# Conv-attention-MoE layer on one core: folded transform, idle matmuls, row spread moved in a DMA queue, a new order at the end

## The chip, the cores and the metric

One NeuronCore of a Trainium2 chip runs the whole layer in one launch; the other cores are idle. The metric is the device time of one execution in microseconds (us), taken as the median of several executions; lower is better. The engines named below are TensorE (PE: matmuls, and PEld: its weight loads), VectorE (DVE), ScalarE (ACT), GpSimd (POOL) and SyncE (SP), which here only issues transfers. Each engine works through its own instructions in order and waits on semaphores for the others.

## What is computed

Four images x of 192 channels by 16 x 16 pixels, all float32. In short (the helper functions are those of the reference):

```python
x = conv(x)              # fft2 over the view [B,16,16,192], first 9 columns of modes kept,
                         # two complex block layers (8 blocks of 24) with relu and softshrink,
                         # irfft2, plus x
t = to_tokens(x)                                   # [4, 256, 192]
t = t + attention(layernorm(t))                    # 12 heads of 16
t = t + moe(layernorm(t))
x = from_tokens(t)                                 # [4, 192, 16, 16]

def moe(xf):
    shared = expert(xf, swg, swu, swd)             # silu(x@wg) * (x@wu) @ wd, 192 -> 384 -> 192
    probs = softmax(xf @ w_gate + expert_bias)     # 16 experts
    p, i = top_k(probs, 2); p = p / sum(p)
    return shared + sum_k p_k * expert_{i_k}(xf)
```

## The kernel before

The program is written by hand, engine by engine, in four stages. Between engines there are only semaphores; the order in each engine's block is the order of execution.

**Transform and convolution (0 to 34 us).** PE multiplies the pixels by a table of cosines and sines (`fwd`, 128 x 576) to get the modes of each image: for each of 8 units `u`, 8 matmuls with 144 columns (L1112), two halves `k` of the 256 pixels accumulated. Then follow the block layers (L1126, L1140, L1145), the inverse transform (L1160), the turn into tokens (L1172), a bias row `out_bias` (L1249) that needs nine small transfers `ld_attn`, and the projections of attention. SP issues all the set-up transfers one after the other, from L412 to L454, between 0.7 and 29.3 us; the last of `ld_attn` is the expert bias at L448. DVE negates the imaginary halves of the weights `w1` and `w2` (L814) after the second image; PE waits for that (`negated`) before L1126.

**Attention (41 to 121 us).** A quad is 4 heads of one image, 12 quads in all. Queries and keys are projected two quads at a time (`project_pair(p)`), ACT adds their bias (`dense_rows(p)`, L677, semaphore `dense_ready`), and SP then copies them with `spread_rows(p)` (L481) from a dense layout into every second row of `qk_sb`. Quad 0 takes a short way; pair 0 serves quads 1 and 2, pair 1 serves quads 3 and 4, and so on. `spread_rows(p)` is in SP's queue between the loads of the expert weights, which are 14.2 MB in 6 groups of gate and up weights (`load_gate_up`, L464) and 4 groups of down weights (`load_down`, L468). PE's loop runs `n` over 24 half quads: scores of half quad `n` (L1296), then the row maxima of half quad `n + 3` (`pair_for_max`, L1267), then other work. So the maxima of half quad 6, the first of quad 3, are taken in iteration `n = 3`, and there PE waits for the rows of `spread_rows(1)`. DVE reduces each bank of maxima (L860), PE transposes them (`maxima_rows`, L1281), DVE shifts the queries.

**Routing (121 to 142 us).** Logits, the two best experts, a rank of each token inside its expert (`rank_and_count`, `base`), a chain of DVE instructions up to `is_part` (L999), then `slot_tokens` (L1473) and the first gathers. The shared expert is computed in 6 units of gate and up matmuls (`shared_gate_up(u)`, L1430 with all 128 rows and L1435 with the 64 that remain; units 0 to 2 for the first two images); pieces of units 0 to 2 stand between the steps of the routing.

**Experts and tail (142 to 243 us).** A loop over tiles of 128 slots, then units 3 to 5 of the shared expert, `shared_down` (L1444), and the reading back of the routed rows (`read_back`, 8 transfers from SP and ACT). For each of 8 token tiles DVE adds two weighted rows to the tokens (`mix`, L1079 and L1081), adds the shared part (`shared_rows`, L976), PE transposes the sums (`out_columns`, L1597, 16 transposes), ACT copies them out of PSUM (L798) and SP stores each image (L509).

The lines of SP's queue on which most depends are these:

```python
load_gate_up(*GU_GROUPS[0])      # experts 0 to 2, 1.77 MB
load_down(*DN_GROUPS[0])         # experts 0 to 3, 1.18 MB
spread_rows(0)
sp.wait_ge(S["tok_ready"], B)
load_down(*DN_GROUPS[1])         # experts 4 to 7, 1.18 MB
spread_rows(1)                   # two transfers of 0.13 MB
spread_rows(2)
load_gate_up(*GU_GROUPS[1])
```

Of the kernel before, what the change touches and what calls it, by code (L numbers as in the profile page):

```python
# [55 lines left out]
SPECTRAL = 2 * 2 * 768 + 3 * N + 4 * C + 3 * B * C + GROUPS * 2 * GC + 2 * GROUPS * B * MODES + B * (2 * C + IM - GC) + GROUPS * 129 + 4 * MODES  # L56
# [22 lines left out]
FILL_SET = 2  # L79


def constants():

    h, w = np.meshgrid(np.arange(H), np.arange(W), indexing="ij")
    k1, k2 = np.meshgrid(np.arange(H), np.arange(WF), indexing="ij")
# [13 lines left out]
        forward.reshape(2, 128, 2 * MODES).transpose(1, 0, 2).reshape(128, -1),  # L99
# [15 lines left out]
F_INV = F_FWD + 2 * 2 * MODES  # L115
# [8 lines left out]
def program(nc, a, out):  # L124
    ctx = ExitStack()
    with ctx:
# [51 lines left out]
        pix = carve(B * (2 * C + IM - GC)).rearrange("p (b c) -> p b c", b=B)  # L178
        w1 = carve(GROUPS * 128).rearrange("p (q r o) -> p q r o", q=GROUPS, r=2)
        b1 = carve(GROUPS)  # L180
        fwd = carve(2 * 2 * MODES).rearrange("p (k m) -> p k m", k=2)
# [18 lines left out]
        after_xT = at[0]  # L200
        probs = probs_flat.rearrange("p (s h k n) -> p s h k n", s=2, h=QUAD, k=2)
# [84 lines left out]

        gu_e = lambda e: main[:, bass.ds(e * GU, GU)]
# [6 lines left out]
        names = """ld_fwd ld_const ld_w1 ld_w2 ld_res ld_attn ld_qkv ld_shared ld_gu ld_dn  # L294
# [10 lines left out]
        mixed half_mixed outT_done outT_ready stored""".split()  # L305
# [28 lines left out]
        def shared_down_bank(u):  # L334
            return bank[(3, 1, 7, 6)[u]]

# [58 lines left out]
        def load_pixels(queue, b):  # L395
            queue.dma_start(pix[:, b, 0:2 * C].rearrange("p (k c) -> p k c", k=2),
                            a["x"][b].rearrange("c h w -> (c h w)").rearrange("(k p c) -> p k c", k=2, p=128)).then_inc(ld_pix[b], 16)
# [13 lines left out]
        def _(sp):  # L411
            sp.dma_start(fwd, a["tables_f32"][:, F_FWD:F_INV].rearrange("p (k m) -> p k m", k=2)).then_inc(S["ld_fwd"], 16)  # L412
# [70 lines left out]

            load_gate_up(*GU_GROUPS[0])
            load_down(*DN_GROUPS[0])
            spread_rows(0)
# [20 lines left out]
            for b in range(B):  # L507
                sp.wait_ge(S["outT_ready"], b + 1)
                sp.dma_start(out[b].rearrange("(k p) h w -> p k (h w)", k=2), out_T[0:CH, b]).then_inc(S["stored"], 16)  # L509
            sp.wait_ge(S["stored"], 16 * B)  # L510
# [3 lines left out]
        def _(pool):  # L514
# [3 lines left out]
            nc.gpsimd.memset(pix[:, :, 2 * C:], 0.0).then_inc(S["zeroed"], 1)  # L518
# [107 lines left out]
        def _(act):  # L626
# [169 lines left out]
            for b in range(B):  # L796
                act.wait_ge(S["outT_done"], b + 1)
                act.activation(out_T[0:CH, b, :, :], bank[b][0:CH, :].rearrange("p (k n) -> p k n", k=2), ACT.Copy).then_inc(S["outT_ready"], 1)  # L798
# [3 lines left out]
        def _(dve):  # L802
            vec = nc.vector
            vec.memset(eps_col, EPS).then_inc(S["eps_set"], 1)

            for b in range(B):
# [3 lines left out]
                if b == 1:  # L810

                    for w, loaded, count in ((w1, "ld_w1", 10), (w2, "ld_w2", 9)):
                        dve.wait_ge(S[loaded], 16 * count)
                        vec.tensor_scalar(w[IM:, :, 0, :], w[IM:, :, 0, :], -1.0, None, ALU.mult).then_inc(S["negated"], 1)  # L814
# [260 lines left out]
            def mix(t):  # L1075

                a, b = (tok, tok_b) if t < NT // 2 else (tok_b, tok)
# [8 lines left out]
            for t in range(NT // 2):  # L1086
# [543 lines left out]
```

## Times and profile before

| | before |
|---|---|
| median of 3 executions | 242.12 us (242.01 to 247.29) |
| the profiled execution | span 242.7 us |
| PE busy, share of the span | 93% |
| DVE, ACT, POOL busy | 62%, 47%, 32% |
| chain that ended last, by engine | PE 81%, DVE 6%, DMA 5%, ACT 4%, issue 2% |
| moved by DMA | 27.67 MB, mean 114 GB/s |

The profile is of one execution. A row of the timeline gives the start, the time from the first start to the last end of a merged run of instructions, engine, line, operation and tiles; in square brackets stands the idle time before it and who ended it. A float32 matmul shows as two records. "SPq" and "ACTq" rows are transfers as they are issued; when they land is in the table of DMA issues. PEclk is the granted clock of TensorE in tenths of 2.4 GHz, so that 5 is 1.2 GHz; the chip records only changes, and before the first change the row shows full clock whatever it was.

### The profile page before, as it was taken

What the parts mean: (1) busy time and instruction counts of PE and PEld (TensorE: products, weight loads), DVE (VectorE), ACT (ScalarE), POOL (GpSimd) and SP (SyncE); (2) the same over time, 40 slices, a digit from 0 to 9 for tenths busy, and PEclk for the clock granted to TensorE, in tenths of its full rate; (3) what the DMA queues carried; (4) which work ended last, traced back from release to release, by engine and by line L of the source; (5) the groups of instructions that cost most, each with busy time, mean ns of one, the idle gap of its engine ahead of it and who ended that gap; (6) DMA issues with size and microseconds to landing.
All of it is one profiled execution on the core that took longest, in us unless ns stands there. A gap on an engine that the chain in (4) does not pass through costs nothing.

```text
span 242.7 us, 5781 instructions
## 1 busy us (share of the span) xinstructions
PE 225.0 (93%) x1968; PEld 147.8 (61%) x1968; DVE 150.7 (62%) x353; ACT 113.3 (47%) x199; POOL 76.7 (32%) x119
## 2 busy tenths in 40 slices
PE   2999999599999999999889999999999999998982
PEld 2989876376666667677574655555555555553371
DVE  0217768344888898878767866565666566652383
ACT  0354046134445344434545357575757565655103
POOL 7003007000000072183510344565656565531000
PEclk9999999857999999999999999999999999999999
DMA  7971499900766895900750011111111111211524
GB/s 192 224 165 26 116 295 233 285 16 13 219 177 172 263 265 173 278 14 24 228 134 0 15 50 36 50 49 49 49 49 49 49 49 49 51 32 35 165 99 130
DMA packets 28099, 27.67 MB, mean 114 GB/s; under 512 B 7788, under 2 KB 26796, under 8 KB 28076
## 3 DMA queue, kind: packets, MB, share of 16 engines
q1 hardware_dynamic: 23372, 21.40, 32.4%
q0 software_dynamic: 2304, 4.72, 6.9%
q10 hardware_dynamic: 2400, 1.26, 2.2%
q8 instruction: 13, 0.21, 0.4%
q14 instruction: 10, 0.08, 0.1%
HBM read 22.49 MB, written 3.44 MB: 107 GB/s over the span
## 4 chain that ended last, share of the span: by engine, by line
PE 81%; DVE 6%; DMA 5%; ACT 4%; issue 2%; SPq 0%; ACTq 0%; DVEq 0%
PE grid L1531 11%; PE grid L1296 9%; PE bank L1557 9%; PE grid L1538 7%; PE bank L1314 4%; PE bank L1547 4%; PE bank L1160 3%; PE bank L1331 3%; PE bank L1267 3%; PE grid L1112 3%; DMA main<-main 2%; PE grid L1430 2%; PE bank L1281 2%; PE grid L1444 2%; PE bank L1126 2%
## 5 line engine op out<-in xcount | busy, mean ns | idle before, releaser
L750 ACT ACTIVATE main<-down_all 128x576 f32 x42 | 28.6, 684 | 27.3 <-PE bank L1557 26.1
L1046 DVE COPY main<-main 128x1152 f32 x41 | 31.7, 785 | 15.5 <-issue 13.8
L716 ACT ACTIVATE main<-grid 128x1024 f32<-128x1024 f32 x24 | 24.5, 1023 | 32.2 <-PE grid L1296 32.2
L582 POOL DMA_INDIRECT main<-xhat_rows,main x21 | 26.3, 1254 | 24.6 <-PE bank L1517 12.6
L1531 PE MATMUL grid<-main 128*64 128x384 f32 x160 | 29.8, 488 | 0.3 <-DVE main L1030 0.3
L1267 PE MATMUL grid<-main 32*128 32x256 f32 x132 | 29.8, 434 | 0.0
L1296 PE MATMUL grid<-main 32*128 32x256 f32 x192 | 27.8, 420 | 0.8 <-ACT main L716 0.6
L590 POOL DMA_INDIRECT pair_rows<-main x19 | 20.4, 1072 | 25.6 <-DVE main L1036 23.8
L860 DVE TENSOR_REDUCE main<-grid 128x2 f32<-128x512 f32 x33 | 21.8, 685 | 4.8 <-PE grid L1267 4.1
L1557 PEld LDWEIGHTS bank<-main 128*64 128x64 f32 x228 | 16.3, 136 | 12.3 <-ACT main L750 9.6
L1557 PE MATMUL bank<-main 128*64 128x192 f32 x228 | 22.7, 333 | 0.1
L1296 PEld LDWEIGHTS grid<-main 32*128 32x128 f32 x192 | 17.4, 196 | 7.8 <-issue 6.8
L1267 PE MATMUL bank<-main 32*128 32x256 f32 x60 | 18.7, 435 | 1.5 <-DMA main<-main 1.5
L1030 DVE TENSOR_TENSOR main<-main,grid 128x384 f32<-128x384 f32 x20 | 11.1, 555 | 13.8 <-ACT main L756 13.8
L559 POOL TENSOR_SCALAR main<-main 128x2 f32<-128x2 f32 x3 | 0.7, 221 | 56.6 <-DVE main L842 56.6
L1267 PEld LDWEIGHTS grid<-main 32*128 32x128 f32 x132 | 17.4, 200 | 0.5 <-issue 0.5
L1538 PE MATMUL grid<-main 64*64 64x384 f32 x160 | 17.5, 508 | 0.0
L1531 PEld LDWEIGHTS grid<-main 128*64 128x64 f32 x160 | 12.8, 137 | 7.7 <-issue 4.0
L860 DVE TENSOR_REDUCE main<-bank 128x2 f32<-128x512 f32 x15 | 10.3, 684 | 6.1 <-PE grid L1267 5.5
L1314 PE MATMUL bank<-main 128*32 128x256 f32 x192 | 12.8, 384 | 1.2 <-issue 1.1
L1547 PEld LDWEIGHTS bank<-cf,main 128*128 128x128 f32 x57 | 5.9, 141 | 11.4 <-issue 10.8
L1267 PEld LDWEIGHTS bank<-main 32*128 32x128 f32 x60 | 11.0, 202 | 2.2 <-DMA main<-main 1.7
(200 smaller groups left out, 399.1 us busy)
## 6 DMA issues: line engine op xcount, KB each, us to landing
down_all<-wd SPq DMA_DIRECT2D x4, 1152.0 KB, 9.3
main<-wg SPq DMA_DIRECT2D x4, 576.0 KB, 4.1
main<-wu SPq DMA_DIRECT2D x4, 576.0 KB, 6.2
main<-wg SPq DMA_DIRECT2D x4, 288.0 KB, 7.0
main<-wu SPq DMA_DIRECT2D x4, 288.0 KB, 8.1
main<-main SPq DMA_DIRECT2D x8, 128.0 KB, 2.7
main<-x SPq DMA_DIRECT2D x1, 768.0 KB, 6.2
main<-wg SPq DMA_DIRECT2D x2, 384.0 KB, 3.6
```

The costliest lines, as they stand in the source:

```text
L582: pool.indirect_dma_start(xg[:, t % 2, :], None, xhat_rows, bass.IndirectOffsetOnAxis(ap=slot_token[:, t:t + 1].bitcast(U32), axis=0)).the ...
L590: pool.indirect_dma_start(pair_rows, bass.IndirectOffsetOnAxis(ap=slot_pair[:, t:t + 1], axis=0), y_out[:, t % 2, :], None).then_inc(y_sto ...
L716: act.activation(probs[:, quad % 2, 2 * (n % 2):2 * (n % 2) + 2, :, :].rearrange("p h k n -> p h (k n)"), grid[:, score_banks(n), :], ACT. ...
L750: act.activation(w_dn[:, p, h, :], dn_e(expert(t, h)), ACT.Copy).then_inc(S["w_dn_ready"], 1)
L860: vec.tensor_reduce(negmax[:, g % QUADS, :, 64 * pair + 32 * h + SHIFT_ROW], max_bank(n, h).rearrange("p (q n) -> p q n", q=2), AX.X, ALU. ...
L1046: vec.tensor_copy(w_gu[:, p, h, :], gu_e(expert(t, h))).then_inc(S["w_gu_ready"], 1)
L1267: last = mm(max_bank(n, h)[:, qh * N:qh * N + N], qk_sb[rows, g % (2 * QUADS), 0, 128 * qh:128 * qh + 128], qk_sb[rows, g % (2 * QUADS), 1 ...
L1296: last = mm(grid[:, score_banks(n).start + h, kh * N:kh * N + N], qk_sb[rows, g % (2 * QUADS), 1, 128 * kh:128 * kh + 128], q_shifted[rows ...
L1314: last = mm(attend_bank(quad)[32 * h:32 * h + 32, 0:N], v_sb[:, b % 2, kh, QUAD * j + h, :], probs[:, s, h, kh, :], start=(kh == 0), stop= ...
L1531: mm(bank[2 * m + p][HALF * h:HALF * h + HALF, 0:FF], xgT[:, p, m, HALF * h:HALF * h + HALF], w_gu[:, p, h, m * FF:(m + 1) * FF], start=Tr ...
L1538: last = mm(bank[2 * m + p][HALF * h:HALF * h + HALF, 0:FF], xgT[rows, p, 1 - m, HALF * h:HALF * h + HALF], w_gu[rows, p, h, 2 * FF:], sta ...
L1557: last = mm(bank[6][HALF * h:HALF * h + HALF, 0:C], hiddenT[:, 128 * f + HALF * h:128 * f + HALF * h + HALF], w_dn[:, p, h, f * C:(f + 1) ...
```

## The change

Six edits are made together.

1. **Idle matmuls.** DVE first sets 128 x 512 bf16 zeros (`idle_rows`), and PE starts with 8 matmuls of 512 columns on them, whose result is overwritten.
2. **Folded transform.** DVE forms the sum and the difference of the two pixel halves of each image (`fold`, two instructions of 128 x 192 for each image). Even rows of modes need only the sum, odd ones only the difference, so each of the 64 matmuls has 72 columns, not 144, and nothing is accumulated; the table is half as large. Both negations of DVE now stand behind all four copies of the spectrum.
3. **SP's queue.** `spread_rows(0)` stands ahead of the first weight groups. And PE's first `maxima_rows` waits for the bias step of pair 0 (`dense_ready` 2), no more for pair 1 and the values.
4. **Routing.** Pieces of shared units 0 and 1 are moved up between `tokens_for_experts(3)`, `gate_logits(3)`, `rank_and_count` and `base`.
5. **Tail.** ACT weights the first routed row (`first_share`), one DVE instruction a tile adds the second. PE transposes the tokens with their shared part and the routed sum apart and adds them in PSUM: 32 transposes instead of 16. The odd read-backs are issued before the second SiLU.
6. **Last image.** ACT copies one half and DVE the other, and two queues store the halves.

The core of the diff:

```diff
@@ SP
+            spread_rows(0)
             load_gate_up(*GU_GROUPS[0])
             load_down(*DN_GROUPS[0])
-            spread_rows(0)
             sp.wait_ge(S["tok_ready"], B)
             load_down(*DN_GROUPS[1])
             spread_rows(1)
@@ ACT
-            for u in range(FC, 2 * FC - 1):
-                shared_silu(u)
+            shared_silu(FC)
             act.wait_ge(S["scattered"], 1)
             for t in range(1, NT, 2):
                 read_back(act, t)
+            shared_silu(FC + 1)
+            for t in range(SHARES_AHEAD):
+                first_share(t)
             shared_silu(2 * FC - 1)
+            for t in range(SHARES_AHEAD, NT):
+                first_share(t)
@@ DVE
+            vec.memset(idle_rows, 0.0).then_inc(S["idle_set"], 1)
...
+            def fold(b):
+                dve.wait_ge(ld_pix[b], 16)
+                for y, op in enumerate((ALU.add, ALU.subtract)):
+                    vec.tensor_tensor(folded[:, b, y * C:(y + 1) * C], pix[:, b, 0], pix[:, b, 1], op).then_inc(S["folded_ready"], 1)
...
+            fold(0)
+            fold(1)
+            for b in range(B):
+                if b + 2 < B:
+                    fold(b + 2)
+                spectrum_columns(b)
+            negate(w1, "ld_w1", 10)
+            negate(w2, "ld_w2", 9)
...
-                dve.wait_ge(back[t], 16)
-                vec.scalar_tensor_tensor(a[:, t, :], y_back[:, t, 0, :], weight[:, t, 0:1], b[:, t, :], ALU.mult, ALU.add).then_inc(S["half_mixed"], 1)
-                dve.wait_ge(S["half_mixed"], t + 1)
-                vec.scalar_tensor_tensor(b[:, t, :], y_back[:, t, 1, :], weight[:, t, 1:2], a[:, t, :], ALU.mult, ALU.add).then_inc(S["mixed"], 1)
+                dve.wait_ge(S["share_ready"], t + 1)
+                vec.scalar_tensor_tensor(y_back[:, t, 1, :], y_back[:, t, 1, :], weight[:, t, 1:2], y_back[:, t, 0, :], ALU.mult, ALU.add).then_inc(S["mixed"], 1)
@@ PE
+            pe.wait_ge(S["idle_set"], 1)
+            for _ in range(IDLE):
+                mm(bank[2 * B - 1][:, 0:512], idle_rows[:, 0:128], idle_rows, start=True, stop=True)
...
                         for r in range(2):
-                            last = mm(bank[u][IM * r:IM * r + IM, q * MODES:(q + 1) * MODES], pix[:, b, col:col + IM],
-                                      fwd[:, k, r * MODES:(r + 1) * MODES], start=(k == 0), stop=(k == 1))
+                            last = mm(bank[u][IM * r:IM * r + IM, at_mode:at_mode + MODES // 2], folded[:, b, col:col + IM],
+                                      fwd[:, y, r, :], start=True, stop=True)
...
             def maxima_rows(g):
                 pe.wait_ge(S["smax_ready"], 4 * g + 4)
-                wait_evicted()
-                if g:
+                if g == 0:
+                    pe.wait_ge(S["dense_ready"], 2)
+                else:
                     pe.wait_ge(S["shift_ready"], g)
...
             tokens_for_experts(3)
+            shared_gate_up(0, second, range(0, 1))
             gate_logits(3)
-            shared_gate_up(0, second, range(0, 1))
+            shared_gate_up(0, second, range(1, 2))
+            shared_gate_up(1, first, range(0, 1))
             rank_and_count()
-            shared_gate_up(0, second, range(1, 2))
+            shared_gate_up(1, second, range(0, 1), opens=False)
             base()
-            shared_gate_up(1)
+            shared_gate_up(1, range(2), range(1, 2))
...
+            for b in range(B // 2):
+                out_columns(b, own, True)
+            pe.wait_ge(S["hid_s_ready"], FC + low.stop)
+            for u in range(NT // 4, NT // 2):
+                shared_down(u, low)
             for b in range(B // 2):
                 pe.wait_ge(S["mixed"], 2 * b + 2)
-                out_columns(b)
+                out_columns(b, routed, False)
+            pe.wait_ge(S["hid_s_ready"], FC + high.stop)
+            for u in range(NT // 4, NT // 2):
+                shared_down(u, high)
+            for b in range(B // 2, B):
+                pe.wait_ge(S["mixed"], 2 * b + 2)
+                out_columns(b, routed, True)
             for b in range(B // 2, B):
                 pe.wait_ge(S["shared_ready"], b + 1)
-                out_columns(b)
+                out_columns(b, own, False)
```

SP's queue behind the set-up transfers, before. `main<-main` is `spread_rows` (first pair 0, then pair 1, then the four of pair 2), `wg`, `wu` and `wd` are expert weights:

```order
L464 DMA main<-wg 128x3x384
L464 DMA main<-wu 128x3x384
L464 DMA main<-wg 64x3x384
L464 DMA main<-wu 64x3x384
L468 DMA down_all<-wd 128x12x192
L481 DMA main<-main 64x2x256 x2
L468 DMA down_all<-wd 128x12x192
L481 DMA main<-main 64x2x256 x2
```

and in the changed kernel, where the line numbers are its own:

```order
L492 DMA main<-main 64x2x256 x2
L475 DMA main<-wg 128x3x384
L475 DMA main<-wu 128x3x384
L475 DMA main<-wg 64x3x384
L475 DMA main<-wu 64x3x384
L479 DMA down_all<-wd 128x12x192 x2
L492 DMA main<-main 64x2x256 x2
L492 DMA main<-main 64x256 x4
```

The rows of pair 0 now leave first. Those of pair 1 and 2 have the same place as before behind the same three weight groups, but these groups can be issued only once pair 0 is ready.

PE's rows in the routing, before, from the last matmul of the ranks (L1458) over the `base` pair (L1465, L1467) to `slot_tokens` (L1473):

```order
L1458 MATMUL bank<-main,cb 128x16
L1435 MATMUL grid<-main,shared_gu 128x256 x2
L1465 MATMUL bank<-cb,main 128x128
L1467 MATMUL bank<-main,cb 16x64
L1430 MATMUL grid<-main,shared_gu 128x512 x2
L1435 MATMUL grid<-main,shared_gu 128x512 x2
L1430 MATMUL bank<-main,shared_gu 128x256 x2
L1435 MATMUL bank<-main,shared_gu 128x256 x2
L1473 MATMUL bank<-main 128x32 x16
```

and in the changed kernel (L1501, L1508, L1510 and L1516 are the same steps, L1473 and L1478 the shared unit's matmuls):

```order
L1501 MATMUL bank<-main,cb 128x16
L1473 MATMUL grid<-main,shared_gu 128x256 x2
L1508 MATMUL bank<-cb,main 128x128
L1510 MATMUL bank<-main,cb 16x64
L1478 MATMUL grid<-main,shared_gu 128x512 x2
L1473 MATMUL bank<-main,shared_gu 128x256 x2
L1478 MATMUL bank<-main,shared_gu 128x256 x2
L1516 MATMUL bank<-main 128x32 x16
```

A first piece of unit 1 (128x256 x2) now stands between the ranks and `base`, in the place of the second piece of unit 0, and less shared work is left between `base` and `slot_tokens`.

PE's last rows, before:

```order
L1430 MATMUL grid<-main,shared_gu 128x512 x2
L1435 MATMUL grid<-main,shared_gu 128x512 x2
L1430 MATMUL grid<-main,shared_gu 128x512 x2
L1435 MATMUL grid<-main,shared_gu 128x512 x2
L1444 MATMUL bank<-shared_dn,main 128x192 x12
L1597 MATMUL grid<-cf,tok_b 96x128 x16
```

and in the changed kernel (L1487 is `shared_down`, L1643 a transpose of `out_columns`):

```order
L1473 MATMUL grid<-main,shared_gu 128x512 x2
L1478 MATMUL grid<-main,shared_gu 128x512 x2
L1643 MATMUL bank<-cf,tok_b 96x128 x8
L1487 MATMUL bank<-shared_dn,main 128x192 x8
L1643 MATMUL bank<-cf,main 96x128 x8
L1487 MATMUL bank<-shared_dn,main 128x192 x4
L1643 MATMUL grid<-cf,main 96x128 x8
L1643 MATMUL grid<-cf,tok_b 96x128 x8
```

The 16 transposes at the end became 32, half of them ahead of the last `shared_down`.

## Rows read from the trace of the kernel before

**Rows 1.** Page, 40 equal slices: granted clock in tenths, and GB/s moved.
```profile
PEclk9999999857999999999999999999999999999999
GB/s 192 224 165 26 116 295 233 285 16 13 219 177 172 263 265 173 278 14 24 228 134 0 15 50 36 50 49 49 49 49 49 49 49 49 51 32 35 165 99 130
```

**Rows 2.** Timeline of the transform: start, us, engine, line, tiles, xcount.
```profile
4.67 6.50 PE L1112 MATMUL grid<-main 128*64 128x144 f32 x64 [4.67 <-DMA main<-x]
10.99 4.10 PE L1112 MATMUL bank<-main 128*64 128x144 f32 x64
...
11.70 0.46 DVE L814 TENSOR_SCALAR main<-main 64x256 f32<-64x256 f32 x2
...
20.42 1.14 PE L1145 MATMUL grid<-main 128*64 128x48 f32 x32
...
34.78 0.35 DVE L932 TENSOR_TENSOR bproj_all<-grid,main 128x192 f32<-128x192 f32 x1
```

**Rows 3.** Timeline and DMA issues (last number: us to landing), end of SP's set-up.
```profile
25.95 0.59 SPq L448 DMA_DIRECT2D wgate<-expert_bias x1
...
wgate<-expert_bias SPq DMA_DIRECT2D x1, 8.0 KB, 3.2
...
32.84 1.24 PE L1249 MATMUL grid<-main 128*128 128x192 f32 x6
```

**Rows 4.** Timeline, the row spread, the maxima and PE behind them.
```profile
41.09 1.27 SPq L481 DMA_DIRECT2D main<-main  x2
...
41.81 2.49 DVE L860 TENSOR_REDUCE main<-grid 128x2 f32<-128x512 f32 x4 [0.75 <-PE grid L1267]
...
47.35 0.79 PE L1267 MATMUL bank<-main 32*128 32x256 f32 x1 [1.50 <-DMA main<-main]
...
61.05 0.48 PE L1267 MATMUL bank<-main 32*128 32x256 f32 x1
```

**Rows 5.** Busy us by engine in four stretches, then PEclk, DMA share, GB/s.
```profile
44.40:47.30 2.90, 0.42 (x3) 0.20 (x2) 0.42 (x1) 0.84 (x2) 0.00 (x0) 0.96 1.02 312
47.30:58.50 11.20, 11.15 (x58) 8.06 (x58) 4.30 (x7) 3.24 (x4) 0.00 (x0) 0.55 0.14 48
58.50:60.90 2.40, 2.29 (x34) 1.29 (x33) 1.09 (x2) 1.86 (x3) 0.00 (x0) 1.00 0.12 27
60.90:63.90 3.00, 3.00 (x26) 1.96 (x26) 2.90 (x8) 1.02 (x1) 0.00 (x0) 1.00 0.58 149
```

**Rows 6.** Timeline of weight transfers, first group and a later one, with landings.
```profile
29.31 0.50 SPq L464 DMA_DIRECT2D main<-wg  x1
...
31.99 1.49 SPq L468 DMA_DIRECT2D down_all<-wd  x1
...
down_all<-wd SPq DMA_DIRECT2D x1, 1152.0 KB, 13.7
...
79.50 0.59 SPq L464 DMA_DIRECT2D main<-wg  x1
...
82.04 0.60 SPq L468 DMA_DIRECT2D down_all<-wd  x1
...
down_all<-wd SPq DMA_DIRECT2D x1, 1152.0 KB, 10.4
```

**Rows 7.** Timeline of PE in the routing.
```profile
126.99 1.11 PE L1430 MATMUL grid<-main,shared_gu 128*128 128x256 f32 x4
...
130.11 0.23 PE L1465 MATMUL bank<-cb,main 16*128 16x128 bf16 x1
...
135.38 0.57 PE L1473 MATMUL bank<-main 128*128 128x32 f16 x16 [0.26 <-DVE main L999]
```

**Rows 8.** Timeline of PE in the tail.
```profile
230.70 2.87 PE L1444 MATMUL bank<-shared_dn,main 128*128 128x192 f32 x16
...
234.59 1.57 PE L1444 MATMUL bank<-shared_dn,main 128*128 128x192 f32 x8 [1.03 <-DVE main L972]
...
238.19 1.11 PE L1597 MATMUL grid<-cf,tok_b 128*96 128x128 f32 x8 [1.16 <-DVE tok_b L976]
```

More of the change, by code:

```diff
@@ L285, in read_back, with store_half @@
                             pair_rows[TOPK * TILE * t:TOPK * TILE * (t + 1), :].rearrange("(p k) c -> p (k c)", k=TOPK)).then_inc(back[t], 16)
+        def store_half(queue, k):
+            queue.dma_start(out[B - 1].rearrange("(k p) h w -> k p (h w)", k=2)[k], out_T[0:CH, B - 1, k]).then_inc(S["stored"], 16)
         gu_e = lambda e: main[:, bass.ds(e * GU, GU)]
@@ L335, in shared_down_bank, with outT_bank @@
             return bank[(3, 1, 7, 6)[u]]
+        def outT_bank(b, k=0):
+            return bank[2] if b == B - 1 and k else bank[(4, 5, 1, 3)[b]]
         def x2T_bank(b):
@@ L506, in _ @@
                 read_back(sp, t)
-            for b in range(B):
+            for b in range(B - 1):
                 sp.wait_ge(S["outT_ready"], b + 1)
                 sp.dma_start(out[b].rearrange("(k p) h w -> p k (h w)", k=2), out_T[0:CH, b]).then_inc(S["stored"], 16)
-            sp.wait_ge(S["stored"], 16 * B)
+            sp.wait_ge(S["outT_ready"], B)
+            store_half(sp, 0)
+            sp.wait_ge(S["stored"], 16 * (B + 1))
         @block.gpsimd
@@ L1435, in shared_gate_up @@
                         last = mm(bank[shared_banks(u)[m]][:, cols], shared_gu[rows, 2 * FF + 128 * f:2 * FF + 128 * f + 128],
-                                  x2T[rows, batch, 1 - m, :], start=False, stop=True)
+                                  x2T[rows, batch, 1 - m, :], start=False, stop=True, skip_group_check=(u == 1))
                         if images.stop == 2:
@@ L1591, in _, with out_columns @@
             shared_gate_up(FC + 2)
-            def out_columns(b):
+            def out_columns(b, rows_of, begins):
                 for k in range(2):
                     for h in range(2):
-                        last = tr(bank[b][0:CH, 256 * k + 128 * h:256 * k + 128 * h + 128], tok_b[:, 2 * b + h, k * CH:(k + 1) * CH], ident)
-                last.then_inc(S["outT_done"], 1)
-            for parts in (low, high):
-                pe.wait_ge(S["hid_s_ready"], FC + parts.stop)
-                for u in range(NT // 4, NT // 2):
-                    shared_down(u, parts)
+                        last = mm(outT_bank(b, k)[0:CH, 256 * k + 128 * h:256 * k + 128 * h + 128], rows_of(2 * b + h)[:, k * CH:(k + 1) * CH], ident,
+                                  is_transpose=True, start=(begins and h == 0 and (k == 0 or b == B - 1)), stop=not begins, skip_group_check=True)
+                if not begins:
+                    last.then_inc(S["outT_done"], 1)
+            own = lambda t: tok_b[:, t, :]
+            routed = lambda t: y_back[:, t, 1, :]
+            for b in range(B // 2):
[3 more added lines that the diff above has]
+                shared_down(u, low)
             for b in range(B // 2):
                 pe.wait_ge(S["mixed"], 2 * b + 2)
-                out_columns(b)
+                out_columns(b, routed, False)
[5 more added lines that the diff above has]
+                out_columns(b, routed, True)
             for b in range(B // 2, B):
                 pe.wait_ge(S["shared_ready"], b + 1)
-                out_columns(b)
+                out_columns(b, own, False)
 _NAMES = {"x": "x", "w1": "L0_conv_w1", "b1": "L0_conv_b1", "w2": "L0_conv_w2", "b2": "L0_conv_b2",
```

69 lines of the change are left out of this document (40 added, 29 removed).

## Prediction

> **What bounds the kernel now.** I read the page first: PE is busy almost everywhere and the chain of waits runs 81% over it, so time is lost only where PE runs empty or slow. The slices show one such place, 42 to 55 us, where the granted clock falls to tenths of 8, 5 and 7 [rows 1]. The timeline there names the cause: SP issues the rows of pair 0 at 41.1, behind 2.9 MB of weights, and PE gets them at 47.35 [rows 4]. In the stretch 44.4 to 47.3 PE is busy for 0.42 of 2.9 us, and in the next 11.2 us it works at a mean clock of 0.55 [rows 5], that is mostly at 1.2 GHz of 2.4. Then I read the two ends and the routing, in the timelines.
>
> **Start.** Before: 64 matmul records take 6.50 us (102 ns each) and the next 64 take 4.10 (64 ns) [rows 2]. The printed clock is full in both, but it can't be: the work is the same, so the first ones ran at the lower clock, before the first recorded change. After: the first fold costs one DVE instruction, 0.35 us by the add of 128 x 192 [rows 2], so the transform starts at 4.67 + 0.35 = 5.0. The smaller table may land a few tenths earlier; I don't count it. A record with 48 columns takes 1.14/32 = 36 ns [rows 2], and I take that for 72 columns, since 64 columns of weights load for each in both. Warm, 128 records take 4.6 us; if the idle matmuls bring nothing, half of them take 51 ns (half of 102) and the sum is 5.6. Then come a spectrum copy and a negation, 0.75 together (both negations are 0.46 [rows 2]; the copy is of like length). L1126 starts at 10.4 to 11.4 instead of 15.0, a gain of 3.6 to 4.6 us. But SP's set-up queue doesn't get faster: the expert bias is issued at 25.95 and lands 3.2 later, at 29.15, and `out_bias` at 32.84 waits for it [rows 3]. So the start can give at most 32.84 - 29.15 = 3.7. **I take -3.6**, bounds -2.8 and -3.7.
>
> **Row spread and clock.** With -3.6, pair 0 is issued at 37.5. The ring is empty then, so the rows land within about 3 us, and PE waits instead for the fourth maximum reduction, which ended at 41.81 + 2.49 = 44.3 [rows 4] and now ends at 40.7. `maxima_rows` takes 0.5, so PE takes up the maxima of half quad 2 at 41.2, not 47.35. The old wait is gone and the clock holds. But what is late next? The weights now leave from 38.8 on, and the rows of pair 1 stand in the same queue behind three groups, 1.77 + 1.18 + 1.18 = 4.13 MB. Before, two of these groups moved while PE did the set-up work (first issue 29.31 [rows 6]); now all three move in the attention loop. PE needs pair 1 in iteration 3: 41.2 + 0.9 (eight maxima records at full clock, half of the 0.42 us a pair at the low one) + 2.4 + 3.0 + 2.4 for iterations 0 to 2 by the durations of the like ones [rows 5] = 49.9. When do they land? A group of three experts with four down weights, issued at 79.50 to 82.04, landed at 82.04 + 10.4 = 92.4 [rows 6], 12.9 us from its first issue. The third group and the rows, 1.18 + 0.26 MB, add 4.9 at the 295 GB/s of the busiest slice [rows 1]. So 38.8 + 12.9 + 4.9 = 56.6. The slow bound is the same group at the start: 31.99 + 13.7 - 29.31 = 16.4 [rows 6] (0.86 MB of shared weights were ahead of it), and 1.44 MB at the slice's 233 GB/s [rows 1] is 6.2: 61.4. I take 56.6, whose conditions (a nearly empty ring, the attention loop running) are the nearest.
>
> So PE stands for 56.6 - 49.9 = 6.7 us in iteration 3. Before, it reached this point at 61.05 [rows 4]: the gain there is 4.4, of which 3.6 is the start's. After an idle time of over twice 2.9 us the clock will have fallen again. What a low clock costs: the 11.2 us from 47.3 did what at full clock is 0.9 + 2.4 + 3.0 = 6.3 by the rows above [rows 5], so 4.9 were lost. How long it lasts this time I can't read; I take a bit less than half of it, **+2.2**, bounds 0 and +4.9. Sum of both: **-4.4 + 2.2 = -2.2**.
>
> The order of the ring decides this. In the Trainium skill, "DMA: Bandwidth & Descriptors", section "Queues, rings and completion order", each DMA engine consumes the descriptors of one ring in order. By that rule nothing small overtakes the weights; the trace agrees, as far as the wait of pair 0 until 47.35 behind the first groups goes [rows 4]. If the rule failed here, the rows would land at once, which is the first rival.
>
> **Routing.** The pieces fill waits, but not the last one. A piece of 4 records takes 0.85 to 1.1 us [rows 7]. One of them now stands between the ranks and `base`, where PE waited for DVE only a short time: PE ends the ranks at about 129.6, so `base` goes at 130.5 instead of 130.11 [rows 7]. Everything behind it is DVE's chain up to `slot_tokens`, at 135.38 before [rows 7], and moves with it. PE's wait there was 0.26. Now it has 8 full-size records' worth left to do, about 2.9 us from 130.5 to 133.4, and `slot_tokens` comes at 135.8: the wait grows to about 2.4, because the work that filled it was moved ahead. Nothing behind `slot_tokens` gets shorter. **+0.4**, bounds -0.3 and +0.8.
>
> **Tail.** DVE's chain gets shorter (16 mixing instructions become 8), so it no longer sets the end; PE does. From 230.70 [rows 8]: 32 transposes at 8 in about 1.0 (1.11 with the drain [rows 8]) = 4.0, `shared_down` 2.7 and 1.4 without their drains [rows 8]: 238.8, against 238.19 + 1.11 = 239.3. The half eviction and the halved last store may give 0.2 and 0.3 more. **-1.0**, bounds -1.8 and +0.3. The trace has no accumulating transpose; I price it as a plain one, and no dearer form is near. In the Trainium skill, "TensorE: Matmul & The Clock Gate", Part 4, a transpose in a kernel is put at about 275 ns; by that, 16 more would cost 4.4 us and the tail would be 1.4 slower than before. The row here, 8 in 1.11 us, speaks for pipelined ones and decides.
>
> **Sum.** 242.7 - 4.4 + 2.2 + 0.4 - 1.0 = 239.9 in a profiled execution. That is the span; the median of the runs shown is 0.6 lower, so 239.3.
>
> **Rivals.**
> - *The second wait doesn't form (rows of pair 1 arrive by 49.9, or a short wait leaves the clock up).* For it: the ring is not always this slow: transfers reached 312 GB/s while PE was idle [rows 5]; my iteration times may be too short. Against it: 4.39 MB in the 11 us from 38.8 would need 400 GB/s, more than any slice shows [rows 1]. Time: 61.05 - 49.9 = 11.1 gained, 242.7 - 11.1 + 0.4 - 1.0 - 0.6 = 230.4; with half of the wait left, about 234. Chance 0.20.
> - *The weights move at their slow pace (slower than before).* Rows land at 61.4: 242.7 + 0.4 + 2.2 + 0.4 - 1.0 - 0.6 = 244.1, with a low clock for the whole 10 us 246.8. It decides from 59.4 on, where the sum passes 242.1. For it: the first group did need 16.4. Against: that time holds 0.86 MB of other loads. Chance 0.13.
> - *PE's longer wait ahead of `slot_tokens` drops the clock.* 2.4 us with nothing is near the 2.9 us with 0.42 busy, after which it fell [rows 5]; PE then works 6 us to the first tile, and half clock would cost up to 3 of them: 242.3. Chance 0.10.
> - *As forecast*: 239.3, its own range 236 to 242. Chance 0.57.
>
> **Chances.** A difference of 2%, 4.8 us, is about what a measurement of this kernel can tell from no change; faster means below 237.3. The first rival gives 0.20 to it, and the lower part of the forecast's range (a landing at 54 or a clock that is back soon) 0.18: 0.38. Slower, above 247, needs the second rival with the long low clock: 0.04. Within 2%: 0.58. The range leaves out half of the first rival and the end of the second: 232 to 244.
>
> **What would show it.** Start: L1126's successor row near 10.4 to 11.4, and the matmul of `out_bias` near 29.2, waiting on a DMA. Row spread: L1309 (the maxima) starts at 41.2 with the clock up; in iteration 3 it has an idle time of some 6 us put down to a DMA `main<-main`, and the granted clock is at 0.5 after it. Routing: L1516 0.4 later than its distance to the end of attention before, with over 2 us idle ahead of it. Tail: PE without gaps from the last gate and up matmuls on. I am wrong above all if the wait of iteration 3 is under 2 us, or if the low clock lasts longer than 10 us.

## The result and the profile after

The changed kernel takes 242.72 us (median of 20 executions, 240.54 to 245.09) against 241.75 us (20 executions, 239.08 to 247.29) for the kernel before: ratio 1.008, 95% interval 1.005 to 1.011. A ratio, here and below, is taken over the executions within 1.5% of each kernel's fastest, and this leaves out 8 of the 20 executions of the kernel before but only 2 of the changed one. By this measure the changed kernel is a little slower; over all 20 executions of each the means are 242.7 and 242.2 us, a difference too small to tell from none beside a spread of 8 us in the kernel before. Either way the forecast gain did not come.

The profiled execution of the changed kernel has a span of 239.6 us and took 241.4 us, so **a time stands 1.8 us above its span** (1.8 to 1.9 in the profiled executions of all later runs). That one sentence decides much of what follows: the execution of before that I had read, span 242.7, was not one of 242.1 us but, by this offset, of about 244.5.

The slices of the changed kernel on the page (granted clock in tenths of 2.4 GHz):

```profile
PEclk9999999995999999999999999999999999999999
```

The dip of the clock is still there, with its lowest slice one later than in [rows 1]. The timeline of the changed kernel (start, us, engine, line) shows the places of which the prediction spoke:

```profile
29.36 1.21 PE L1291 MATMUL grid<-main 128*128 128x192 f32 x6 [0.50 <-DMA wgate<-expert_bias]
...
41.11 0.48 PE L1309 MATMUL bank<-main 32*128 32x256 f32 x1
...
56.46 0.79 PE L1309 MATMUL grid<-main 32*128 32x256 f32 x1 [4.93 <-DMA main<-main]
...
133.38 0.57 PE L1516 MATMUL bank<-main 128*128 128x32 f16 x16 [2.17 <-DVE main L1039]
...
227.61 1.13 PE L1478 MATMUL grid<-main,shared_gu 64*128 64x512 f32 x4
```

The first row answers to the last of [rows 3]: the bias row waits for SP's transfer. The second and third answer to the last two of [rows 4]: PE has the rows of pair 0 at 41.1 instead of 47.35, and then stands 4.93 us in iteration 3 for those of pair 1. The fourth answers to the last of [rows 7]: the wait ahead of the slot tokens is 2.17 instead of 0.26. The timeline of SP's queue in the same stretch, and then the windows, with the busy time of PE, PEld, DVE, ACT and POOL, clock, DMA share and GB/s in the wait and behind it:

```profile
37.48 1.33 SPq L492 DMA_DIRECT2D main<-main  x2
38.85 0.60 SPq L475 DMA_DIRECT2D main<-wg  x1
...
41.40 4.38 SPq L479 DMA_DIRECT2D down_all<-wd  x2
45.83 8.46 SPq L492 DMA_DIRECT2D main<-main  x6
```

```profile
51.30:56.40 5.10, 0.23 (x3) 0.00 (x0) 0.80 (x2) 1.02 (x1) 0.00 (x0) 0.75 1.00 305
56.40:60.70 4.30, 4.24 (x14) 2.67 (x14) 1.51 (x3) 0.00 (x0) 0.00 (x0) 0.50 0.83 244
```

The DMA engines are full (share 1.00) while PE is nearly empty (0.23 of 5.10 us), and PE then works at 1.2 GHz, as in most of the second stretch of [rows 5]. The issue of the rows is held up too: six issues take SP 8.46 us, and the longest of them 5.2 us, so the second transfer of pair 1 was issued only at about 51.

### The profile page after: what moved, and what is told of

Read it like the earlier page. It is cut to its first block, busy times and chain, and to the rows that moved or that the text cites. A ratio compares the mean times of both kernels' runs of the same rounds, so it can differ in the third digit from the quotient of the medians.

```text
span 239.6 us, 5835 instructions
## 1 busy us (share of the span) xinstructions
PE 222.5 (93%) x1996; PEld 144.3 (60%) x1996; DVE 150.7 (63%) x355; ACT 115.8 (48%) x207; POOL 76.7 (32%) x119
## 4 chain that ended last, share of the span: by engine, by line
PE 77%; SPq 11%; DMA 4%; issue 3%; ACT 2%; DVE 2%; DVEq 0%
PE grid L1576 11%; PE bank L1602 9%; PE grid L1339 8%; PE grid L1583 7%; PE grid L1473 4%; PE bank L1592 4%; PE bank L1357 3%; PE bank L1374 3%; PE grid L1309 3%; PE bank L1261 2%; SPq L438 2%; PE bank L1309 2%; DMA main<-main 2%; PE bank L1324 2%; PE grid L1478 2%
## 5 line engine op out<-in xcount | busy, mean ns | idle before, releaser
L1309 PE MATMUL grid<-main 32*128 32x256 f32 x132 | 28.1, 409 | 4.9 <-DMA main<-main 4.9
L1339 PE MATMUL grid<-main 32*128 32x256 f32 x192 | 26.0, 398 | 0.7 <-ACT main L729 0.6
L1339 PEld LDWEIGHTS grid<-main 32*128 32x128 f32 x192 | 16.3, 184 | 7.3 <-issue 6.6
L1309 PEld LDWEIGHTS grid<-main 32*128 32x128 f32 x132 | 16.5, 188 | 6.1 <-DMA main<-main 5.3
L1309 PE MATMUL bank<-main 32*128 32x256 f32 x60 | 17.7, 416 | 0.0
L1576 PEld LDWEIGHTS grid<-main 128*64 128x64 f32 x160 | 12.8, 137 | 7.8 <-issue 3.8
L1357 PE MATMUL bank<-main 128*32 128x256 f32 x192 | 12.8, 384 | 1.3 <-issue 1.1
L1592 PEld LDWEIGHTS bank<-cf,main 128*128 128x128 f32 x57 | 5.9, 141 | 11.4 <-issue 10.8
L907 DVE TENSOR_TENSOR main<-bank,main 128x256 f32<-128x256 f32 x12 | 5.1, 421 | 11.2 <-PE bank L1324 11.2
## 6 DMA issues: line engine op xcount, KB each, us to landing
down_all<-wd SPq DMA_DIRECT2D x4, 1152.0 KB, 10.2
```

The lines of the kernel that those rows point to most:

```text
L1309: last = mm(max_bank(n, h)[:, qh * N:qh * N + N], qk_sb[rows, g % (2 * QUADS), 0, 128 * qh:128 * qh + 128], qk_sb[rows, g % (2 * QUADS), 1 ...
L1339: last = mm(grid[:, score_banks(n).start + h, kh * N:kh * N + N], qk_sb[rows, g % (2 * QUADS), 1, 128 * kh:128 * kh + 128], q_shifted[rows ...
L1357: last = mm(attend_bank(quad)[32 * h:32 * h + 32, 0:N], v_sb[:, b % 2, kh, QUAD * j + h, :], probs[:, s, h, kh, :], start=(kh == 0), stop= ...
L1576: mm(bank[2 * m + p][HALF * h:HALF * h + HALF, 0:FF], xgT[:, p, m, HALF * h:HALF * h + HALF], w_gu[:, p, h, m * FF:(m + 1) * FF], start=Tr ...
```

## The experiments

Each kernel was timed beside the kernel before on the same chip; a ratio is to that. The runs were spread over three chips, so medians of different experiments can come from different chips; the fastest executions of the kernel before were 239.0, 238.5 and 238.8 us on the three. Two parts of the change have no run of their own: the folded transform and the last image's halves. What the fold gives is read from the start of the traces, and the halves were only taken out together with the rest of the tail.

### The kernel before once more

No edit.

> The kernel before, profiled once more and timed against itself. Theory A: the profiled execution of before (span 242.7 us, low clock from 47.1 to 57.3) was one of the slower of its kind, since the time of a run stands 1.8 us above its span in the runs of the changed kernel (241.4 for a span of 239.6), while the median of 20 runs of before is 241.75, which is a span of about 240.0. Then another profile has a span of 238 to 241 and the low clock in the row spread's stretch lasts 3 to 7 us, not 10. Theory B: the profiled execution was typical and the offset between span and time differs between the kernels; then a span of 242 to 243 and a time of about 242 come out again.

Measured: median 240.14 us, ratio 1.002 (0.999 to 1.005). Its profiled execution has a span of 237.6 us (time 239.4), and the clock does not fall before 235 us. PE takes up the maxima of half quad 2 at 45.99 without a wait, where in [rows 4] it waited 1.50 us until 47.35. The slices of its page, and its timeline:

```profile
PEclk9999999999999999999999999999999999999997
```

```profile
45.65 0.41 PE L1281 MATMUL bank<-cf,main 128*128 128x128 f32 x2 [1.03 <-ACT main L677]
45.99 0.48 PE L1267 MATMUL bank<-main 32*128 32x256 f32 x1
```

Theory A holds, and more than it said: the kernel before has no single time here. Of the 58 executions of it that ran in these experiments, on three chips, with their mean granted clock over the span:

| mean clock | executions | mean time, range |
|---|---|---|
| 0.987 and more | 24 | 239.5 (238.5 to 240.3) |
| 0.980 to 0.987 | 10 | 242.7 (241.5 to 244.2) |
| under 0.980 | 24 | 245.9 (243.8 to 248.3) |

Of the changed kernel's 20 executions none is in the first row: 8 lie at 0.983 to 0.986 (mean 241.4), 5 at 0.979 (242.8) and 7 under that (244.0). Over all 58 and all 20 the means are both 242.7. So the change takes away the best executions and the worst. (The limits between the rows of the table are mine. A real gap in the times lies only between the first row and the rest, from 240.3 to 241.5; from there to 248.3 they go on without one.) Why PE gets the rows at 46.0 in one execution and at 47.35 in the other, I can say only in part: the two row transfers land 3.0 and 3.8 us after their issue in the one, 3.0 and 5.6 in the other.

### Two weight groups behind the rows of pair 1

```diff
             spread_rows(0)
             load_gate_up(*GU_GROUPS[0])
+            spread_rows(1)
             load_down(*DN_GROUPS[0])
             sp.wait_ge(S["tok_ready"], B)
-            load_down(*DN_GROUPS[1])
-            spread_rows(1)
             spread_rows(2)
+            load_down(*DN_GROUPS[1])
```

> Changed kernel, with SP's queue re-ordered: rows of pair 0, gate and up group 0, rows of pair 1, down group 0, rows of pair 2, down group 1. So 2.36 MB less stand ahead of the rows of pair 1. Theory ring order: these rows land at about 47 instead of 56.4, the wait of 5.1 us in iteration 3 is gone and the clock does not fall there; the span is 5 to 8 us below 239.6, and the median ratio to before is 0.965 to 0.98. Rival, bandwidth or something else limits iteration 3: a wait of over 3 us remains and the time stays within 1% of the changed kernel's.

Measured: 234.61 us, ratio 0.978 (0.972 to 0.984). The trace has no wait of PE for `main<-main` and no low clock in attention, only one in the routing (128.1 to 131.5). But the rows did not land at 47, as I had expected. They were issued from 43.12 on and landed 7.0 us later (median of the two), the second at about 51, because the last transfer of the weight group ahead of them landed only at 50.4. PE takes them up at 51.95, with less than 1 us to spare.

A landmark in the chains of work is the first output projection (start, us, engine, line). In the first profile of the kernel before:

```profile
78.56 1.95 PE bank L1331 x12
```

In its second profile:

```profile
72.94 1.95 PE bank L1331 x12
```

In the changed kernel:

```profile
76.00 1.95 PE bank L1374 x12
```

And in this one:

```profile
69.46 1.95 PE bank L1374 x12
```

The changed kernel is 2.6 us ahead of the disturbed execution of before, but 3.1 behind the clean one, and 6.5 behind the same kernel with two groups of weights moved. The last figure is too small, because that execution came to attention late: its bias row starts at 30.77, not at 29.36, and its maxima of half quad 2 at 42.51, not at 41.11:

```profile
42.51 0.48 PE L1309 MATMUL bank<-main 32*128 32x256 f32 x1
```

From these maxima to the landmark it is 69.46 - 42.51 = 26.95 us here, 72.94 - 45.99 = 26.95 in the second profile of before, and 76.00 - 41.11 = 34.89 in the changed kernel. So the second wait with its low clock cost 7.9 us. Of these, 4.9 are the idle time, 2.0 come behind the maxima of half quad 6 at the low clock, and 1.0 is there because PE works off the scores of half quad 3 (1.13 us) ahead of the wait, where here they run beside the maxima.

### One weight group behind them

```diff
             load_down(*DN_GROUPS[0])
             sp.wait_ge(S["tok_ready"], B)
-            load_down(*DN_GROUPS[1])
             spread_rows(1)
             spread_rows(2)
+            load_down(*DN_GROUPS[1])
```

> Changed kernel, with only the last of the three weight groups (down weights of experts 4 to 7, 1.18 MB) put behind the rows of pairs 1 and 2. A dose between the changed kernel (4.13 MB ahead of pair 1, rows there at 56.4, idle 4.9 us) and the kernel with 1.77 MB ahead (no idle time). Theory ring order: 1.18 MB at the 360 GB/s of that stretch are 3.3 us, so the rows are there at 53, PE's idle time ahead of the maxima of half quad 6 is 1.5 to 2.5 us, and the span is 2 to 4 us below 239.6. Rival, the wait has another cause: idle time and span stay.

Measured: 236.28 us (4 executions), ratio 0.985 (0.974 to 0.996), span of the profiled one 232.7. The wait is all but gone (0.15 us, from 50.86 to 51.01); I had expected 1.5 to 2.5 us to be left. The first of the two row transfers is issued at 41.42 and lands 9.1 us later, the second is there at about 51, which is just when PE comes to them. Counted from the issue of the first weights, the rows are there after 17.6 us in the changed kernel (56.4 - 38.85), after 12.8 here (51.0 - 38.18) and after about 10.8 with two groups moved (51.1 - 40.26). So the dose acts in the expected direction but not in proportion: the first 1.18 MB is worth 4.8 us of the landing, not 3.3, and the second about 2.0.

### The rows of pair 1 on another queue

```diff
             dense_rows(1)
+            act.wait_ge(S["dense_ready"], 4)
+            act.wait_ge(S["odd_rows_set"], 2)
+            for part in range(2):
+                act.dma_start(qk_sb[0:128:2, 3:5, part, :], dense[64 * part:64 * part + 64, 1, 0:2, :]).then_inc(spread_qk[1], 16)
```

with `spread_rows(1)` taken out of SP's queue.

> Changed kernel, but the rows of pair 1 are issued by ScalarE, on its own queue, right behind the bias step of pair 1; all weight groups stay where they are. Theory ring order: on another queue the rows do not stand behind the weights, they land within 2 to 4 us of their issue (by 46) although just as many bytes move, the idle time in iteration 3 is gone and the span is 232 to 235. Rival, the DMA engines themselves are full and the order does not matter: the rows land after 52 and the idle time stays over 2 us.

Measured: 236.47 us (4 executions), ratio 0.985 (0.976 to 0.994), span 234.9. All weights stay where they were, and yet PE's wait in iteration 3 shrinks from 4.9 to 0.4 us (waits by releaser: us, times, longest; then the DMA issues):

```profile
PE grid L1312 <- DMA main<-main: 0.4, 1, 0.4
```

```profile
main<-main ACTq DMA_DIRECT2D x2, 128.0 KB, 8.8
```

It is the place behind the weights in SP's queue that makes the rows late, since the same bytes move. But the rows still need 8.8 us (median of the two) and PE gets them at 51.53 rather than the expected 46: beside full DMA engines a queue of its own did not make 0.26 MB fast. The Trainium skill ("DMA: Bandwidth & Descriptors", section "Queues, rings and completion order") says that the engines take queues in turns and each queue in its order. The trace agrees so far: the rows, issued at 41.31, were there before the down weights that SP had issued at 41.08, which landed 11.7 us later, at 52.8. How large a turn is, it does not show.

### The old order of the queue

```diff
-            spread_rows(0)
             load_gate_up(*GU_GROUPS[0])
             load_down(*DN_GROUPS[0])
+            spread_rows(0)
```

> Changed kernel, with SP's queue in the old order (rows of pair 0 behind gate and up group 0 and down group 0). Theory: pair 0 lands at about 46 to 47 as before, because it is bound by the weights ahead of it and not by the start, so the start's 3.5 us are lost there and the time is that of before, less 0.5 for tail and routing: ratio 0.99 to 1.00. If moving the rows was what cost time, the ratio is under 0.985; if the move was worth something, over 1.005 (that is, over the changed kernel's 1.008).

Measured: 241.2 us, ratio 1.003 (0.998 to 1.008), span 240.0. With the shorter start, but the weights ahead of pair 0, PE waits where it had waited before, for longer:

```profile
43.62 0.48 PE L1309 MATMUL bank<-main 32*128 32x256 f32 x1 [2.98 <-DMA main<-main]
```

The rows landed at 43.6, earlier than the 46 to 47 I had expected, so the start's gain is not lost whole: PE takes up the maxima 2.4 us earlier than in the second profile of before. The clock then fell in attention (45.3 to 52.1) and once more in the routing (130.6 to 137.4). Against the changed kernel (1.008) the intervals overlap, and the ratio lies between the two limits that I had set (0.985 and 1.005): with the short start, moving the rows neither helped nor hurt by an amount that can be told.

### The third edit alone, in the kernel before

```diff
+            spread_rows(0)
             load_gate_up(*GU_GROUPS[0])
             load_down(*DN_GROUPS[0])
-            spread_rows(0)
...
                 pe.wait_ge(S["smax_ready"], 4 * g + 4)
-                wait_evicted()
-                if g:
+                if g == 0:
+                    pe.wait_ge(S["dense_ready"], 2)
+                else:
```

> The kernel before, with the third edit alone: pair 0's rows ahead of the first two weight groups, and the first maxima rows not waiting for pair 1. Theory: pair 0 is there at once, but the weights start at 42.4 and the rows of pair 1 land 17.5 us later (56.4 - 38.9 in the changed kernel), at 60, while PE needs them at about 54.5; an idle time of 4 to 6 us and a low clock of 7 to 10 us follow in every execution, the span is 241 to 244 and the median about 244, that is not better than the kernel before and worse than its executions without low clock (239.0 to 240.3). Rival: the move is a gain by itself and the start's part is lost elsewhere; then the median is 240 or less.

Measured: 250.01 us (6 executions, 246.15 to 251.32), ratio 1.034 (1.020 to 1.048). PE stands 4.23 us for pair 1, until 59.0 (expected 60), and the clock falls there (58.9 to 65.8) and again in the routing (127.2 to 137.4):

```profile
59.00 0.79 PE L1267 MATMUL grid<-main 32*128 32x256 f32 x1 [4.23 <-DMA main<-main]
```

The move by itself is a clear loss, 6 us larger than I expected. The second low clock explains only part of it: against the second profile of before (237.6), this execution (248.4) has lost 6.8 us by the first output projection and 3.9 more up to the slot tokens. What brings the low clock in the routing stays open. What the whole change loses by the move, its start and tail for the most part give back.

### The old order of the routing

In the changed kernel, and then in the one with two weight groups moved:

```diff
             tokens_for_experts(3)
-            shared_gate_up(0, second, range(0, 1))
             gate_logits(3)
-            shared_gate_up(0, second, range(1, 2))
-            shared_gate_up(1, first, range(0, 1))
+            shared_gate_up(0, second, range(0, 1))
             rank_and_count()
-            shared_gate_up(1, second, range(0, 1), opens=False)
+            shared_gate_up(0, second, range(1, 2))
             base()
-            shared_gate_up(1, range(2), range(1, 2))
+            shared_gate_up(1)
```

> Changed kernel, with the routing's order of before alone. Theory: base comes 0.4 to 0.6 us earlier against the end of attention, and the idle time ahead of the slot tokens goes back from 2.2 to about 0.3 us; span 0.4 to 0.6 us shorter, ratio to before about 0.002 lower than the changed kernel's 1.008. Rival: the pieces did fill waits and the time grows by 0.5 us.

> The kernel with SP's queue re-ordered (median 234.6), with the routing's order of before. Theory: executions at full clock are 0.4 to 0.6 us shorter (233.6 becomes 233.1), since base comes earlier; the idle time of 2.2 us ahead of the slot tokens goes. Rival, from the run of the changed kernel with the old routing (ratio 1.0185, low clock from 123.4 to 130.2 in its profile): the old order has its idle time ahead of the logits and sees a low clock there in more executions, and the median is 1 to 3 us longer.

Measured: in the changed kernel 244.05 us, ratio 1.019 (1.012 to 1.025); in the other one 233.61 us, ratio 0.977 (0.970 to 0.983), against 234.61 and 0.978. In both traces the wait ahead of the slot tokens is back at 0.3 us (the second one, 2.2 before):

```profile
124.58 0.56 PE L1516 MATMUL bank<-main 128*128 128x32 f16 x16 [0.26 <-DVE main L1039]
```

The two disagree. In the changed kernel the old order is 1% slower, with a low clock from 123.4 to 130.2 in its profile and mean clocks of 0.965 to 0.972 in all six executions; in the other kernel it is 1.0 us shorter in the median, with the fastest executions at 232.4 and 232.7 against 233.6, though on another chip and with overlapping intervals. The work term is there in the trace: from the first output projection to the slot tokens it takes 124.58 - 67.75 = 56.8 us instead of 126.83 - 69.46 = 57.4; what decides the clock in the routing stays open.

### The wait ahead of the slot tokens filled

```diff
             shared_gate_up(2, first)
+            shared_gate_up(2, second)
             slot_tokens()
             tile_experts()
-            shared_gate_up(2, second)
```

> The kernel with SP's queue re-ordered (median 234.6), and in the routing the second piece of shared unit 2 moved ahead of the slot tokens. Theory: PE stands idle for 2.2 us ahead of the slot tokens in the changed kernel; 1.7 us of the work that now stands behind them fits in, so the wait is 0.5 us and the span 1.5 to 1.7 us shorter (median about 233), with fewer low-clock stretches in the routing. Rival: something else (the gather, the weight copies) sets the first tile and the time stays within 0.3 us.

Measured: 233.99 us, ratio 0.975 (0.968 to 0.983), against 234.61. The first wait shrinks to 0.48, but a new one of 1.09 us comes behind it, on DVE's product of the shared unit:

```profile
125.28 0.57 PE L1516 MATMUL bank<-main 128*128 128x32 f16 x16 [0.48 <-DVE main L1039]
...
127.06 4.45 PE L1487 MATMUL grid<-shared_dn,main 128*128 128x192 f32 x16 [1.09 <-DVE main L1012]
```

The 0.6 us in the median is less than the intervals can tell, and the trace shows no gain: from the slot tokens to the last gate and up matmuls it takes 222.24 - 125.28 = 97.0 us here and 222.69 - 126.83 = 95.9 without the filling, with 3.4 us of low clock in both. The clock fell here too (128.2 to 131.6), with 0.48 and then 1.09 us idle instead of 2.17 at once; so the long wait is not needed for a low clock there.

### Without the idle matmuls

```diff
-IDLE = 8
+IDLE = 0
```

> The kernel with SP's queue re-ordered (median 234.6), without the 8 idle matmuls. Theory: the transform's end moves 1 to 2 us later (L1154 starts at the same time, at the low clock), but the bias row at 29.2 to 29.4 waits for SP's transfer all the same, so the span changes by less than 0.3 us. Rival: the clock later in the kernel or the first stages depend on it and the span grows by 1 us or more.

Measured: 234.88 us, ratio 0.983 (0.975 to 0.991), against 234.61: no difference that can be told. The first 64 transform records take 4.05 us instead of 2.87, but the bias row starts at 29.51 against 29.36:

```profile
4.77 4.05 PE L1154 MATMUL grid<-main 128*64 128x72 f32 x64 [4.77 <-DVE main L836]
...
29.51 1.24 PE L1291 MATMUL grid<-main 128*128 128x192 f32 x6
```

### The old tail

The kernel with the filled routing and the ends of all four engine blocks (and of the stores) from the kernel before, in short:

```diff
-            for b in range(B // 2):
-                out_columns(b, own, True)
...
             for b in range(B // 2):
                 pe.wait_ge(S["mixed"], 2 * b + 2)
-                out_columns(b, routed, False)
+                out_columns(b)
```

> The kernel with SP's queue re-ordered and the routing's wait filled (median 234.0), with the tail of before. Theory: from the last gate and up matmuls to the end it takes 12.0 us as in the kernel before, against 10.9 in the changed one, so the time is 1.1 us longer. Rival: the 16 more transposes cost what the rest gives, and the time is the same within 0.3.

Measured: 235.43 us, ratio 0.983 (0.976 to 0.989), against 233.99. That is 1.4 us in the median; the intervals overlap, but the traces agree on the direction. From the last gate and up matmuls to the end this kernel takes 234.5 - 220.5 = 14.0 us and the one with the new tail 234.2 - 222.2 = 12.0; the changed kernel takes 239.6 - 227.6 = 12.0, and the kernel before 242.7 - 229.6 = 13.1 in its first profile and 237.6 - 224.0 = 13.6 in its second. The old tail varies by a wait of `shared_down` for DVE, which was 1.03, 1.55 and 1.91 us in these three traces; the new tail has none. Eight transposes took 1.04 to 1.08 us in the changed kernel, the adding ones as well.

## Why the prediction was wrong

The predicted 239.3 us and the forecast of a small gain rest on a sum against one profile, and as a forecast of a profile the sum was close: 239.9 predicted, 239.6 measured. Step by step, against the profile of [rows 1 to 8]:

| step | predicted | measured |
|---|---|---|
| start, at the bias row | -3.6 | 29.36 - 32.84 = -3.5 |
| maxima of half quad 2 | 41.2 | 41.11 |
| landing of pair 1 | 56.6 | 56.4 |
| PE idle in iteration 3 | 6.7 | 4.93 (5.9 with the scores that no longer run beside the maxima) |
| maxima of half quad 6 | -4.4 | 56.46 - 61.05 = -4.6 |
| low clock behind it | +2.2 | 53.9 to 60.7; the lead falls from 4.6 to 2.6: +2.0 |
| routing | +0.4 | 2.17 us idle; +0.6 |
| tail | -1.0 | -1.1 |

PE stood from 51.5, not from 49.9. Iterations 0 to 2 took 0.7 us longer than I had priced them (51.95 - 42.51 = 9.44 us to the same maxima in the kernel with two groups moved, against 8.7), and the scores of half quad 3 came before the wait. The landing came as worked out from another group of weights. The +2.2 was luck: the prediction itself says that it could not read how long the low clock would last and took a bit less than half of 4.9.

**The step that failed is the last one, "the median of the runs shown is 0.6 lower".** I subtracted the median of three executions from the span of a fourth as if the difference were an offset. The offset is +1.8, and the profiled execution was one of about 244.5 us, 2.7 above the median of 20: its clock fell at the end of the wait for pair 0 and stayed low for 10.2 us. With +1.8 the sum would have said 241.7 for one execution; the changed kernel's profiled one took 241.4 and its median is 1.3 above that. And I counted the removal of that wait and of that low clock as a gain for all executions. The second profile of before shows what the change is up against in the others: no wait for pair 0, no low clock there, 239.4 us. Against that profile the same change comes out as a loss of 2.0 us of span (237.6 to 239.6):

| stretch | changed kernel less the second profile of before |
|---|---|
| start, up to the maxima of half quad 2 | 41.11 - 45.99 = -4.9 |
| from there to the first output projection | 34.89 - 26.95 = +7.9 |
| routing, up to the slot tokens | 57.4 - 56.8 = +0.6 |
| tail | 12.0 - 13.6 = -1.6 |

Of the -4.9, 3.7 are there at the bias row (33.05 to 29.36); ahead of the maxima the kernel before also waits 1.03 us for the bias step of pair 1, which the third edit takes out. The changed kernel seems to bring the second wait in every execution: the three traces with all three weight groups ahead of pair 1 and pair 0 in front show it with 4.93, 4.21 and 4.23 us, and none of the 20 timed executions has a mean clock above 0.986. The three times shown, 242.01 to 247.29, were a warning: 5 us between executions of one kernel is larger than every term of my sum.

The rivals: the first (no second wait) did not come in the changed kernel, but moving two weight groups made it, at 234.6. Its forecast of 230.4 was too low by the same offset: 230.4 plus 2.4 is 232.8, and the fastest executions are at 233.6, with the old routing at 232.4. The second rival (slow weights) did not occur; the result lies on its side of no change all the same. The third (a low clock in the routing) was given 0.10, and a low clock there was seen in the profiles of seven other kernels of this study, with long and with short waits ahead of it, but not in that of the changed kernel.

The version to keep is the changed kernel with `spread_rows(1)` ahead of the first and `spread_rows(2)` ahead of the second group of down weights, with the old routing: 233.6 us, ratio 0.977 to the kernel before and some 9 us below the changed kernel (on another chip). With the new or the filled routing, and without the idle matmuls, it is the same within what was measured.

## What to carry to other kernels

- Whoever moves a small transfer forward in a queue has to ask where the large ones go. Here they could be issued only behind it and came to stand in front of the next small one, and a wait of 1.5 us in one execution and none in another became one of 4.9.
- Before a sum is made against one profile, find out where that execution stands among the others, by its span plus the offset between span and time; when executions of a kernel differ by more than the terms of the sum, a second profile is worth more than a finer sum.
- A wait behind which the clock falls in some executions and not in others costs by its share, and a gain there has to be counted so.

## What I had not expected of the hardware

The executions of one kernel are of two kinds on each of three chips: 24 of 58 lie within 2 us (238.5 to 240.3), with a mean granted clock of 0.988 or more, and the others spread from 241.5 to 248.3 with one of 0.986 or less. A low clock, once begun, was kept for some us though PE was busy again (53.9 to 60.7 in the changed kernel, 4.24 us of work in the 4.30 behind the wait). And three ways of bringing the rows of pair 1 forward, with one weight group behind them, with two, or on ScalarE's queue, all had them there at about 51: while the DMA engines are full, transfers of 0.13 MB took some 7 to 9 us from issue to landing. An issue can be held up as well, here for 5.2 us, when much stands in the queue.
